# The first token group's routing moved from the start of a routed-experts stage into the attention stage before it

## The chip, the cores and the metric

The kernel runs on one core of a Trainium2 chip. The metric is the device time of one execution in microseconds; less is better. The engines are TensorE (PE, with its weight loads as PEld), VectorE (DVE), ScalarE (ACT), GpSimd (POOL) and SyncE (SP), which here only issues transfers.

## The reference

Four blocks follow each other on x of 32 sequences by 128 tokens by 128 features; each is a cross-attention to a context and a feed-forward part, both added to x with a tanh gate after a layer norm. The kernel's stages 0 to 7 are these eight parts. The change touches stage 2 and stage 3, the second block:

```
x = x + jnp.tanh(g_xattn[1]) * _L1_xattn_ref(_layernorm(x), ctx, ...)   # 16 heads of 8, softmax over 128 keys, then a 2-layer MLP
x = x + jnp.tanh(g_ffn[1]) * _L1_ffn_ref(_layernorm(x), ...)

logits = x @ classifier_weight.T              # 40 experts: 32 routed, 8 identity
scores = softmax(logits)
_, topk_idx = top_k(scores + bias, 6)
topk_w = take_along_axis(scores, topk_idx) * 2.5
out = x * (sum of the weights of the identity experts)
for each of the 32 routed experts:            # intermediate width 64
    gate, up = split(x @ Wgu.T)
    out = out + w[:, None] * (silu(gate) * up @ Wd.T)
```

## The kernel before

x stays on the chip (x_resident), as 8 groups of 4 sequences, 512 tokens each. Each stage is a program block of its own; `end_layer` (L72) closes it with a barrier of all engines. Inside a stage each engine has its own instruction list, written out by hand, and waits on semaphores.

**Stage 2, the attention** (`layer2_attention`). `stream` calls a body for groups 0 to 7 with the group at hand (`at`), the one `before`, the one `after` and the one after that (`after2`). The body has four batches b (one sequence each). TensorE makes scores for batch b + 2, weighs the values of batch b, turns the probabilities of b + 1. VectorE takes the reciprocal of a batch's sums (`invert`, L596), then `shift`: two reduces for the row maxima (L585) and two subtracts (L590) on the scores. ScalarE makes the exponentials, copies the turned probabilities and keeps the outputs; GpSimd multiplies by the reciprocals (L545). In the slots of the batches lie also the norm of `after2` (statistics at b = 1, power on GpSimd at b = 2, normalise at b = 3, turned by TensorE and copied by ScalarE at b = 3), the projections of `after`, and the closing MLP (`hide`, L776, `mix`, L784) and `update` (L603) of `before`. Groups 6 and 7 have no `after2`, group 7 no `after`, so these slots are empty there. All this uses one work bank. After the last group come `hide(LAST)` twice, `mix(LAST)` and `update(LAST)`.

**Stage 3, the routed experts** (`layer3_experts`). `turns` runs over the 8 groups; a group has 16 units u of two experts. TensorE multiplies a unit's gate and up weights with the group's turned normalised rows (L1763), ScalarE applies silu (L1726), VectorE multiplies by up (L1686), GpSimd multiplies by the routing weights of the tokens (L1632), and TensorE, three units later, adds the down-projection into a bank (L1778). GpSimd's operand, `w_spread`, is each expert's row of weights repeated over 64 partitions: the weights are transposed (L1750), copied (L1715), written to a row tensor in DRAM (L1606) and read back with eight broadcast transfers (L1613) in four quarters of four units each; `spread[q]` tells that a quarter is there. The next group's norm (steps 0, 2, 4), router (6), routing chain (7) and spread rows (11) lie inside the group at hand. The first group has none before it: its norm, router, chain of some 25 VectorE instructions and spread stand ahead of everything in the stage. SP issues five weight loads of stage 4 first.

## Time and profile before

| | |
|---|---|
| median of three runs | 2156.19 us (2155.06 to 2162.08) |
| span of the profiled execution | 2160.3 us, 47261 instructions |
| TensorE busy | 1966.5 us, 91% |
| VectorE busy | 1551.1 us, 72% |
| ScalarE busy | 1229.6 us, 57% |
| GpSimd busy | 815.2 us, 38% |
| mean granted TensorE clock | 0.941 |
| stage 2's last update ends, stage 3's first group after it | 933.10 us, to 998.10 us |

The profiled execution's own time is known only as its span, from first to last instruction; it lies 4.1 us above the median of the runs. A busy share is a mean over eight stages with different limits, so what a change in one stage is worth has to be read in the order of time around it. In a timeline row the first number is the start, the second the duration of the merged piece, x the count of instructions in it, and the brackets hold the engine's idle time before it and what ended that.

### The profile page before, as it was taken

What the parts mean: (1) busy time and instruction counts of PE and PEld (TensorE: products, weight loads), DVE (VectorE), ACT (ScalarE), POOL (GpSimd) and SP (SyncE); (2) the same over time, 40 slices, a digit from 0 to 9 for tenths busy, and PEclk for the clock granted to TensorE, in tenths of its full rate; (3) what the DMA queues carried; (4) which work ended last, traced back from release to release, by engine and by line L of the source; (5) the groups of instructions that cost most, each with busy time, mean ns of one, the idle gap of its engine ahead of it and who ended that gap; (6) DMA issues with size and microseconds to landing.
All of it is one profiled execution on the core that took longest, in us unless ns stands there. A gap on an engine that the chain in (4) does not pass through costs nothing. (4 is left out here: it accounts for less than half of the span.)

```text
span 2160.3 us, 47261 instructions
## 1 busy us (share of the span) xinstructions
PE 1966.5 (91%) x18167; PEld 1500.7 (69%) x18167; DVE 1551.1 (72%) x3176; ACT 1229.6 (57%) x2804; POOL 815.2 (38%) x708
## 2 busy tenths in 40 slices
PE   6879999999995999969999995997998999999986
PEld 3669999999894666636666663776685666666676
DVE  6899999999987989835444436765586666666656
ACT  2498888888861777713323323884522666666642
POOL 4344454544461333224445444442000333333333
PEclk7699999999997999979999998997999999999995
DMA  2000000000002000043454330001000000000001
GB/s 89 19 2 14 8 15 8 14 15 8 14 2 81 9 9 6 2 97 79 98 123 97 79 80 19 12 1 56 0 2 8 5 5 5 5 5 5 1 1 41
DMA packets 41566, 61.67 MB, mean 29 GB/s; under 512 B 9624, under 2 KB 18368, under 8 KB 40960
## 3 DMA queue, kind: packets, MB, share of 16 engines
q1 hardware_dynamic: 41344, 58.66, 11.2%
q8 instruction: 146, 2.39, 0.5%
q14 instruction: 76, 0.62, 0.1%
HBM read 56.03 MB, written 2.62 MB: 27 GB/s over the span
## 5 line engine op out<-in xcount | busy, mean ns | idle before, releaser
L916 POOL TENSOR_TENSOR a_probs<-a_probs,a_rsums 128x1024 f32<-128x1024 f32 x64 | 121.4, 1897 | 351.0 <-DVE a_rsums L964 351.0
L1632 POOL TENSOR_TENSOR f_h<-f_gated,f_w_spread 128x512 f32<-128x512 f32 x128 | 161.7, 1269 | 194.6 <-PE f_acc L1778 87.2
L1686 DVE TENSOR_TENSOR f_gated<-f_silu,f_up 128x512 f32<-128x512 f32 x128 | 86.9, 684 | 183.2 <-PE f_up L1763 171.3
L1726 ACT ACTIVATE f_silu<-f_gate 128x512 f32<-128x512 f32 x128 | 76.4, 597 | 230.3 <-PE f_gate L1763 230.2
L2453 ACT ACTIVATE f_combine<-f_logits,f_neg_row_max 128x128 f32<-128x128 f32 x512 | 198.5, 395 | 1.0 <-DVE f_neg_row_max L2308 1.0
L2281 POOL TENSOR_TENSOR f_slot_sum<-f_slot_sum,f_logits 128x512 f32<-128x512 f32 x96 | 122.8, 1279 | 171.7 <-DVE f_slot_max L2387 137.8
L2289 POOL TENSOR_TENSOR f_acc<-f_acc,f_row_factor 128x512 f32<-128x512 f32 x128 | 136.9, 1071 | 62.2 <-ACT f_logits L2460 40.0
L1778 PEld LDWEIGHTS f_acc<-f_down,f_h 128*128 128x128 f32 x1024 | 128.9, 192 | 42.7 <-issue 37.8
L2518 PE MATMUL f_give_bank<-f_y,f_combineT 128*128 128x128 f32 x1024 | 139.3, 279 | 14.8 <-DVE f_y L2357 9.6
L952 DVE TENSOR_REDUCE a_negmax<-a_score_bank 128x8 f32<-128x1024 f32 x64 | 78.2, 1222 | 94.1 <-PE a_score_bank L1105 93.9
L2545 PE MATMUL f_logit_bank<-f_phi,f_xT 128*128 128x128 f32 x1024 | 138.0, 279 | 3.3 <-ACT f_logits L2433 3.3
L2518 PEld LDWEIGHTS f_give_bank<-f_y,f_combineT 128*128 128x128 f32 x1024 | 125.0, 192 | 21.0 <-DVE f_y L2357 17.7
L2507 PE MATMUL f_slot_bank<-f_logits,f_xn 128*128 128x128 f32 x1024 | 136.2, 276 | 1.0 <-DVE f_logits L2379 1.0
L1778 PE MATMUL f_acc<-f_down,f_h 128*128 128x128 f32 x1024 | 131.8, 275 | 2.6 <-POOL f_h L1632 2.6
L1763 PE MATMUL f_gate<-f_xT,f_gate_up 128*128 128x512 f32 x256 | 132.6, 600 | 0.9
L1763 PE MATMUL f_up<-f_xT,f_gate_up 128*128 128x512 f32 x256 | 131.6, 596 | 0.0
L2545 PEld LDWEIGHTS f_logit_bank<-f_phi,f_xT 128*128 128x128 f32 x1024 | 126.8, 195 | 4.5 <-ACT f_logits L2433 3.5
L2373 DVE TENSOR_TENSOR f_logits<-f_logits,f_neg_slot_max 128x512 f32<-128x512 f32 x128 | 127.6, 997 | 2.1 <-ACT f_combine L2453 2.1
L2507 PEld LDWEIGHTS f_slot_bank<-f_logits,f_xn 128*128 128x128 f32 x1024 | 124.5, 192 | 2.3 <-DVE f_logits L2379 1.2
L2493 PE MATMUL f_expert_bank<-f_w,f_slots 128*32 128x128 f32 x4096 | 125.9, 275 | 0.0
L2493 PEld LDWEIGHTS f_expert_bank<-f_w,f_slots 128*32 128x32 f32 x4096 | 108.6, 110 | 7.9 <-issue 0.2
L1030 ACT ACTIVATE a_probs<-a_probs 128x1024 f32<-128x1024 f32 x64 | 67.7, 1059 | 66.5 <-DVE a_probs L955 66.4
(326 smaller groups left out, 4931.4 us busy)
## 6 DMA issues: line engine op xcount, KB each, us to landing
f_w_spread<-f_routing_rows SPq DMA_DIRECT2D x64, 512.0 KB, 10.2
f_w<-in_f_w SPq DMA_DIRECT2D x16, 256.0 KB, 2.5
a_cT<-in_ctxT SPq DMA_DIRECT2D x16, 192.0 KB, 2.7
f_gate_up<-in_f_guT SPq DMA_DIRECT2D x1, 2048.0 KB, 7.9
out<-x_resident SPq DMA_DIRECT2D x8, 256.0 KB, 2.4
c_cT<-in_ctxT SPq DMA_DIRECT2D x8, 192.0 KB, 2.7
a_ctx<-in_ctx SPq DMA_DIRECT2D x8, 192.0 KB, 2.6
f_phi<-in_f_phi SPq DMA_DIRECT2D x1, 1024.0 KB, 5.5
```

The lines of the kernel that those rows point to most:

```text
L916: nc.gpsimd.tensor_tensor(probs[:, u], probs[:, u], rsums[:, u, :].unsqueeze(2).to_broadcast([S, 8, S]), ALU.mult).then_inc(normalised, 1)
L1632: nc.gpsimd.tensor_tensor(h[:, u % KEPT, :], gated[:, u % 2, :], w_spread[:, u // PER, u % PER, :], ALU.mult).then_inc(weighted, 1)
L1763: nc.tensor.matmul(ps[step % 2][:, :], gu_w[:, step, k, :], norm.xT[:, s, :], start=True, stop=True).then_inc(done, 1)
L1778: last = nc.tensor.matmul(acc[s][:, j * D:(j + 1) * D], h[:, u % KEPT, j * S:(j + 1) * S], down_w[:, u, :], start=u == 0 and j == 0, stop= ...
L2281: nc.gpsimd.tensor_tensor(slot_sum[:, :, :], slot_sum[:, :, :] if g > 1 else raw[:, (m - 1) % RING], raw[:, m % RING], ALU.add).then_inc(p ...
L2289: nc.gpsimd.tensor_tensor(acc[:, group(g), :], acc[:, group(g), :], factor[:, m // GROUPS % 3, group(g)].unsqueeze(2).to_broadcast([S, G, D]),
L2373: nc.vector.tensor_tensor(e, e, wide(neg_slot[:, m // GROUPS % 3, :]), ALU.add).then_inc(shifts, 1)
L2453: last = nc.scalar.activation(back[:, m % BACKS, j, :], raw[:, m % RING, j, :], ACT.Exp, bias=neg_row[:, k, b:b + 1], accum_out=row_part[: ...
L2493: last = nc.tensor.matmul(expert_banks[m % 2][rows, j * D:(j + 1) * D], slots[:, m % KEPT, j, rows], w_s[:, k, e, :], start=True, stop=True)
L2507: last = nc.tensor.matmul(slot_bank[:, j * CH:(j + 1) * CH], norm.xn[:, g, j, :], raw[:, m % RING, j, :], start=True, stop=True)
L2518: last = nc.tensor.matmul(give_banks[m % 2][:, j * D:(j + 1) * D], backT[:, m % TURNED, j, :], y[:, m % KEPT, j, :], start=True, stop=True)
L2545: last = nc.tensor.matmul(logit_banks[m % 2][:, j * CH:(j + 1) * CH], norm.xT[:, g, j * S:(j + 1) * S], phi_c[:, c, :], start=True, stop=True)
```

## The change

The routing's tiles, semaphores and steps move out of `layer3_experts` into a class, `Routing`, which both stages use. For the first token group: the statistics and the setup of the chain go to group 6, b = 1, of the attention; the power to b = 2; normalise, turn and copy to b = 3; the router, logit maximum, shift and exponential to group 7, b = 0; the weights to b = 1; their transposes and the copy to b = 3. They use the attention's work bank, so hide(before, 0) of group 7 waits for the shift, and hide(LAST, 0) for the copy of the turned weights. SP then writes the rows and issues the first two of four spread quarters while still in stage 2; the last two are issued first in stage 3, ahead of stage 4's loads. `w_spread` becomes four tiles, two of which are allocated around both stages, and norm6's buffers are allocated later. The body of `vector_weights` is that of `route` before; the stage's other groups do the same steps as before, through the class.

```diff
+class Routing:
+
+
+
+    ER, EZ, TOP, SCALE = 32, 8, 6, 2.5
+    E, PAD = ER + EZ, 8 - TOP
+    CHAIN = 15
...
+    def vector_start(self):
+        self.nc.vector.memset(self.cand[:, :, :], BIG).then_inc(self.chain, 1)
+        self.nc.vector.tensor_scalar(self.gscale[:, :], self.core.gates[:, 5:6], self.SCALE, None, ALU.mult)\
+            .then_inc(self.chain, 1)
+
+    def tensor_router(self, pe, norm, s, it, bank):
+        pe.wait_ge(norm.xT_ready, it + 1)
+        for j in range(G):
+            last = self.nc.tensor.matmul(bank[:, j * self.E:(j + 1) * self.E], norm.xT[:, s, j * S:(j + 1) * S],
+                                         self.rw[:, :], start=True, stop=True)
+        last.then_inc(self.logits_in, 1)
+
+    def vector_logits(self, dve, it, bank):
+
+        logits = bank[:, 0:G * self.E].rearrange("p (j e) -> p j e", j=G)
+        dve.wait_ge(self.logits_in, it + 1)
+        self.nc.vector.tensor_reduce(self.negmax[:, :], logits, AX.X, ALU.max, negate=True).then_inc(self.chain, 1)
+        dve.wait_ge(self.chain, it * self.CHAIN + 3)
+        self.nc.vector.tensor_tensor(self.shifted[:, :, :], logits, self.wide(self.negmax[:, :]), ALU.add)\
+            .then_inc(self.shift_done, 1)
+
+    def scalar_exp(self, act, it):
+        act.wait_ge(self.shift_done, it + 1)
+        self.nc.scalar.activation(self.exps[:, :, :], self.shifted[:, :, :], ACT.Exp).then_inc(self.exp_done, 1)
+
+    def vector_weights(self, dve, s, it):
...
+        dve.wait_ge(self.exp_done, it + 1)
+        nc.vector.tensor_reduce(self.sums[:, :], self.exps[:, :, :], AX.X, ALU.add).then_inc(chain, 1)
...
+        nc.vector.tensor_reduce(self.wz[:, s, :], self.w[:, s, :, ER:], AX.X, ALU.add).then_inc(self.routed, 1)
+
+    def tensor_turn(self, pe, s, it, bank):
+        pe.wait_ge(self.routed, it + 1)
+        for j in range(G):
+            last = self.nc.tensor.transpose(bank[0:self.ER, j * S:(j + 1) * S], self.w[:, s, j, 0:self.ER],
+                                            self.core.ident[:, :])
+        last.then_inc(self.w_turned, 1)
+
+    def scalar_keep(self, act, s, it, bank):
+        act.wait_ge(self.w_turned, it + 1)
+        self.nc.scalar.activation(self.wT[:, s, :], bank[0:self.ER, :], ACT.Copy).then_inc(self.wT_ready, 1)
+
+    def sync_rows(self, sp, i, s, it):
+        sp.wait_ge(self.wT_ready, it + 1)
+        sp.dma_start(self.rows[s], self.wT[:, s, :]).then_inc(self.rows_out[s], 16)
+        sp.wait_ge(self.rows_out[s], i * 16 + 16)
+
+    def sync_spread(self, sp, s, q, place, per):
+
+        half = 128 // 2
+        rows = self.rows[s, 2 * per * q:2 * per * (q + 1), :].rearrange("(p e) n -> e p n", e=2)
+        for e in range(2):
+            sp.dma_start(place[e * half:(e + 1) * half], rows[e].unsqueeze(0).to_broadcast([half, per, N]))\
+                .then_inc(self.spread[q], 16)
...
+                routing.sync_rows(sp, 0, 0, 0)
+                for q, place in enumerate(spread_first):
+                    routing.sync_spread(sp, 0, q, place[:, :, :], 4)
...
+                        if after and not after2 and b == 2:
+                            next_norm.gpsimd_rstd(pool, *FIRST)
...
                             invert(*((at, b - 1) if b else (before, G - 1)))
                         if after2 and b == 1:
                             norm.vector_stats(dve, *after2)
+                        if after and not after2 and b == 1:
+                            dve.wait_ge(updated, 1)
+                            next_norm.vector_stats(dve, *FIRST)
+                            routing.vector_start()
                         if before and b == 3:
                             update(before)
                         if after2 and b == 3:
                             norm.vector_normalise(dve, *after2)
+                        if after and not after2 and b == 3:
+                            next_norm.vector_normalise(dve, *FIRST)
                         batch = batch_at(at, after, b + 2)
                         if batch:
                             shift(*batch)
                         if after and b == 1:
                             bias_values(after, work_bank)
+                        if not after and b == 0:
+                            routing.vector_logits(dve, 0, work_bank)
+                        if not after and b == 1:
+                            dve.wait_ge(routing.held.landed, routing.held.all)
+                            routing.vector_weights(dve, 0, 0)
                 stream(dve, group)
                 invert(LAST, G - 1)
...
+                        if after and not after2 and b == 3:
+                            next_norm.scalar_copy(act, *FIRST)
                         if batch:
                             copy_turned(*batch, 2)
                             copy_turned(*batch, 3)
...
                             exponentiate(*batch)
+                        if not after and b == 0:
+                            routing.scalar_exp(act, 0)
+                        if not after and b == 3:
+                            routing.scalar_keep(act, 0, 0, work_bank)
                 stream(act, group)
...
+                        if not after and b == 0:
+                            pe.wait_ge(routing.held.landed, routing.held.all)
+                            routing.tensor_router(pe, next_norm, 0, 0, work_bank)
...
+                        if not after2 and b == 3:
+                            pe.wait_ge(updated, before[2] + 1)
+                            if after:
+                                next_norm.tensor_turn(pe, *FIRST)
+                            else:
+                                routing.tensor_turn(pe, 0, 0, work_bank)
...
                         if before and b == 1:
-                            if after:
-                                pe.wait_ge(v_ready, after[2] + 1)
+                            pe.wait_ge(*((v_ready, after[2] + 1) if after else (routing.shift_done, 1)))
                             hide(before, 0)
                         if before and b == 2:
                             mix(before)
                 stream(pe, group)
+                pe.wait_ge(routing.wT_ready, 1)
                 for f in range(2):
                     hide(LAST, f)
                 mix(LAST)
...
                 sp.sem_inc(weighted, 2)
+                for q in range(len(spread_first), QUADS):
+                    routing.sync_spread(sp, 0, q, w_spread[q][:, :, :], PER)
                 load_ahead(sp, ahead)
...
+                def spread_routing(i, s, it):
+                    routing.sync_rows(sp, i, s, it)
...
-
-                spread_routing(0, 0, 0, True)
-                turns(sp, lambda i, s, it, nxt: nxt and spread_routing(*nxt, False))
+                        sp.wait_ge(weighted, (it - 1) * STEPS + (q + 1) * PER + 2)
+                        routing.sync_spread(sp, s, q, w_spread[q][:, :, :], PER)
+                turns(sp, lambda i, s, it, nxt: nxt and spread_routing(*nxt))
...
             def _(pool):
-                norm.gpsimd_rstd(pool, 0, 0, 0)
-
...
-                nc.vector.memset(cand[:, :, :], BIG).then_inc(chain, 1)
-                nc.vector.tensor_scalar(gscale[:, :], core.gates[:, 5:6], SCALE, None, ALU.mult).then_inc(chain, 1)
-                dve.wait_ge(weights, LOADED)
...
-                norm.vector(dve, 0, 0, 0)
-                route(0, 0)
...
-                norm.scalar_copy(act, 0, 0, 0)
-                exp_of(0)
-                keep_routing(0, 0)
...
-                pe.wait_ge(weights, LOADED)
...
-                norm.tensor_turn(pe, 0, 0, 0)
-                router(0, 0)
-                turn_routing(0, 0)
...
+                norm3 = Norm(core, weights3, "f1", None, begun_before=True)
+                routing = Routing(core, weights3, held3)
+                spread_first = [core.sbuf(f"f1_w_spread{q}", [128, 4, N], ctx=weights3) for q in range(2)]
```

## Rows read from the trace of the kernel before

**Rows 1.** Windows: length, busy us of PE, PEld, DVE, ACT, POOL; granted clock, DMA.

```profile
921.00:933.00 12.00, 7.60 (x33) 4.35 (x24) 1.60 (x2) 1.76 (x3) 0.46 (x1) 0.63 0.01 1
933.00:948.00 15.00, 3.85 (x17) 3.14 (x17) 6.49 (x36) 0.93 (x2) 1.24 (x2) 0.50 0.19 64
948.00:958.00 10.00, 8.74 (x17) 3.44 (x16) 2.42 (x10) 4.26 (x6) 0.08 (x1) 0.83 0.64 148
```

**Rows 2.** Timeline over the boundary of stage 2 and 3: start us, us, engine.

```profile
932.35 0.75 DVE L603 SCALAR_TENSOR_TENSOR x_resident<-a_work_bank,gates,x_resident 128x512 f32<-128x512 f32 x1 [9.53 <-PE a_work_bank L784]
...
934.32 0.20 DVE L1640 MEMSET f_cand<- 128x168 f32 x1 [1.22 <-PEq L72]
...
942.27 0.33 DVE L1650 TENSOR_REDUCE f_negmax<-f_norm_bank 128x4 f32<-128x160 f32 x1 [3.89 <-PE f_norm_bank L1743]
...
943.36 0.32 DVE L1654 TENSOR_REDUCE f_sums<-f_exps 128x4 f32<-128x160 f32 x1 [0.40 <-ACT f_exps L1711]
...
947.17 1.03 PE L1750 MATMUL f_turn_bank<-ident,f_w 128*32 128x128 f32 x4 [4.93 <-DVE f_w_identity L1674]
...
948.00 1.91 PE L1763 MATMUL f_gate<-f_xT,f_gate_up 128*128 128x512 f32 x2
...
948.85 0.33 SPq L1606 DMA_DIRECT2D f_routing_rows<-f_wT  x1
...
950.50 5.38 SPq L1613 DMA_DIRECT2D f_w_spread<-f_routing_rows  x8
...
951.98 0.69 DVE L1686 TENSOR_TENSOR f_gated<-f_silu,f_up 128x512 f32<-128x512 f32 x1 [4.87 <-ACT f_silu L1726]
...
957.92 1.26 POOL L1632 TENSOR_TENSOR f_h<-f_gated,f_w_spread 128x512 f32<-128x512 f32 x1 [20.68 <-DMA f_w_spread<-f_routing_rows]
```

**Rows 3.** Timeline of TensorE in stage 3, first token group and start of second.

```profile
959.33 1.13 PE L1778 MATMUL f_acc<-f_down,f_h 128*128 128x128 f32 x8 [2.59 <-POOL f_h L1632]
...
963.63 0.63 PE L173 MATMUL f_norm_bank<-ident,f_xn 128*128 128x128 f32 x4 [1.46 <-DVE f_xn L162]
...
998.10 1.02 PE L1763 MATMUL f_gate<-f_xT,f_gate_up 128*128 128x512 f32 x2
```

**Rows 4.** Timeline of VectorE in the attention's last two token groups.

```profile
880.68 2.35 DVE L585 TENSOR_REDUCE a_negmax<-a_score_bank 128x8 f32<-128x1024 f32 x2 [1.27 <-PE a_score_bank L739]
...
894.85 0.75 DVE L603 SCALAR_TENSOR_TENSOR x_resident<-a_work_bank,gates,x_resident 128x512 f32<-128x512 f32 x1 [1.16 <-PE a_work_bank L784]
895.88 2.35 DVE L585 TENSOR_REDUCE a_negmax<-a_score_bank 128x8 f32<-128x1024 f32 x2 [0.28 <-PE a_score_bank L739]
...
907.64 2.36 DVE L585 TENSOR_REDUCE a_negmax<-a_score_bank 128x8 f32<-128x1024 f32 x2 [0.40 <-PE a_score_bank L739]
...
912.18 0.94 DVE L596 RECIPROCAL a_rden<-a_kept 128x128 f32<-128x128 f32 x1
...
919.55 0.75 DVE L603 SCALAR_TENSOR_TENSOR x_resident<-a_work_bank,gates,x_resident 128x512 f32<-128x512 f32 x1 [2.88 <-PE a_work_bank L784]
```

**Rows 5.** Timeline of TensorE at the entry of the last stage.

```profile
2108.69 0.63 PE L1310 MATMUL f_turn_bank<-ident,f_xn 128*128 128x128 f32 x4 [1.52 <-PEq L72]
```

**Rows 6.** Timeline of VectorE in an ordinary token group of the attention.

```profile
837.89 0.75 DVE L603 SCALAR_TENSOR_TENSOR x_resident<-a_work_bank,gates,x_resident 128x512 f32<-128x512 f32 x1 [1.16 <-PE a_work_bank L784]
...
839.59 2.35 DVE L585 TENSOR_REDUCE a_negmax<-a_score_bank 128x8 f32<-128x1024 f32 x2
...
850.85 0.81 DVE L142 BATCH_NORM_STATS2 a_stats<-x_resident 128x6 f32<-128x128 f32 x4
...
852.20 2.36 DVE L585 TENSOR_REDUCE a_negmax<-a_score_bank 128x8 f32<-128x1024 f32 x2
```

**Rows 7.** Timeline of TensorE at the end of the attention.

```profile
923.41 1.42 PE L776 MATMUL a_work_bank<-a_oT,a_w 128*128 128x512 f32 x2 [2.09 <-POOL a_oT L545]
...
925.61 2.08 PE L776 MATMUL a_work_bank<-a_oT,a_w 128*128 128x512 f32 x2 [0.78 <-ACT a_hT L670]
...
928.46 3.78 PE L784 MATMUL a_work_bank<-a_w,a_hT 128*128 128x128 f32 x16 [0.78 <-ACT a_hT L670]
```

More of the change, by code:

```diff
@@ L1560, in _, with layer3_experts @@
                         expand(LEAD + m // 2)
-def layer3_experts(core, held, ahead):
-    nc, ER, EZ, TOP, I, SCALE = core.nc, 32, 8, 6, 64, 2.5
-    E, PAD = ER + EZ, 8 - TOP
-    STEPS, QUADS = ER // 2, 4
+def layer3_experts(core, norm, routing, spread_first, held, ahead):
+    nc, I = core.nc, 64
+    STEPS, QUADS = Routing.ER // 2, 4
     PER = STEPS // QUADS
@@ L1768, in group @@
                         if nxt and step == ROUTER_AT:
-                            router(nxt[1], nxt[2])
+                            routing.tensor_router(pe, norm, nxt[1], nxt[2], norm_bank)
                         if nxt and step == SPREAD_AT:
-                            turn_routing(nxt[1], nxt[2])
+                            routing.tensor_turn(pe, nxt[1], nxt[2], turn_bank)
                         if step >= DOWN_LAG:
```

146 lines of the change are left out of this document (64 added, 82 removed).

## The prediction

> **What bounds the kernel now.** I read the windows around the boundary of stage 2 and stage 3 first, then the timeline of all engines over it, the start of stage 3 on TensorE, and last VectorE's order of work in the attention's ordinary and last groups.
>
> The 15 us after the attention's last update hold almost nothing: TensorE is busy 3.85 us, VectorE 6.49, ScalarE 0.93, GpSimd 1.24, at a granted clock of 0.50 [rows 1]. What runs there is one chain. The update ends at 933.10, VectorE starts the stage at 934.32, the logits' reduction comes at 942.27, the routing weights from 943.36, their transposes at 947.17, the first gate matmul at 948.00, the first row write at 948.85, the spread transfers from 950.50, and GpSimd's first product at 957.92, after 20.68 us idle, released by the spread transfer [rows 2]. TensorE has by then run four units ahead and idles 2.59 us until that product allows the first down-projection, then 1.46 us more for the second group's normalised rows [rows 3]. From there it is continuous: 998.10 is the second group's first gate. So in this stage TensorE sets the end, and what is late at the start is paid in full at the stage's closing barrier.
>
> In the attention the pace is a loop of scores on TensorE and reduce and subtract on VectorE: VectorE's reduce at 907.64 waits only 0.40 us for TensorE's scores, which wait for the subtract before; two batches lie between 895.88 and 907.64, 5.88 us each [rows 4]. VectorE work put there costs only what exceeds such a gap.
>
> **Removed from the start of stage 3.** TensorE's first gate matmul then waits only for a semaphore (gateds) that VectorE raises as it enters; the turned rows exist already. Stage 2's last update to VectorE's first instruction took 1.22 us [rows 2]; at the entry of the last stage, where TensorE also has work ready, it started at the same 2108.69 as that stage's first VectorE work, 1.52 us idle behind the barrier [rows 5]. I take 934.32 plus an estimated 0.2 us of weight load: gate matmul at 934.5 against 948.00, which is 13.5 us. (Between 934.3, no load, and 935.5, a second barrier's length, the bounds.)
>
> The Trainium skill ("Runtime: NRT & Kernel Launch", Instruction fetch mechanics) says that a branch out of the fetched window makes the sequencer stall for a fetch; before, TensorE waited for the norm at this entry and would have hidden it. The page gives no time for it, and the stage entry in [rows 5] shows none worth counting; by that rule the 13.5 would shrink, by the row it does not.
>
> Then the pipe. Before, the fourth unit ended 2.59 us ahead of 959.33 [rows 3], at 956.7, or 8.7 us after the first gate. GpSimd's first product had its other input at 952.67, when VectorE's first gated tile was done [rows 2], and was late at 957.92 only for its transfer. Without that it comes 4.8 us after the first gate, at 939.3, and ends 1.26 us later at 940.6, ahead of the fourth unit's end, now 943.2. Its transfer must land by 939.3. In the tail: transposes at about 921.4 once the last weighing is done, row write 1.68 us later (947.17 to 948.85), spread issue 1.65 later (950.50), landing no more than 7.42 later (957.92) [rows 2]: 921.4 + 1.0 of slip (below) + 10.75 = 933.2. Six microseconds are spare; each microsecond beyond would cost one. Quarters three and four are issued after the barrier, at 934.3; even at twice 7.42 they land at 949, and unit 8, in the middle of a group that took 50.1 us (948.00 to 998.10), comes near 957. So the 2.59 us go. The 1.46 us go too: statistics, GpSimd's power and the normalise of group 1 depend on the first product, now 2.5 us ahead of the fourth unit instead of 2.6 behind the need; even a normalise slowed to 3 us fits. Sum: 13.5 + 2.59 + 1.46 = 17.55 us. The five loads for stage 4 now stand behind four spread issues in SP's queue (5.38 us for eight [rows 2], so under 3), and are for the stage after this one: nothing.
>
> **Added to the attention.** In group 6, batch 1: four statistics and four aggregations. Ordinary groups have the same at this place: 850.85 to the reduce at 852.20, no idle [rows 6], where group 6 had a 1.27 us gap before 880.68 [rows 4]; 1.35 with overlap fits the gap. The memset and the scale behind it (0.20 and 0.10 long, pitch far less) have no cover left: 0.2 us. GpSimd's two instructions (1.24 us [rows 1]) sit between two products a 5.88 us batch apart: nothing, 1.24 if that cover were gone. Batch 3: the normalise between update and reduce. Ordinary group: 837.89 to 839.59, 1.70 us [rows 6]; group 6: 894.85 to 895.88, 1.03 us [rows 4]. Plus 0.67 us, on the loop. Transposes and ScalarE's copy stand where ordinary groups have them: nothing.
>
> Group 7, batch 0: eight router matmuls between two pairs of turns (all of TensorE's moved work is 3.85 us at the 0.50 clock [rows 1], 1.9 at full; I estimate half of it for the router), in the time VectorE takes for its reduce and subtract; the turns behind them come later by a few tenths and the chain over ScalarE's copies may pass some on. I count 0.1. The two logit instructions (0.33 us each, 942.27 [rows 2]) delay the last subtract by 0.3 after the 0.40 us gap, but TensorE has a full queue of turns, weighing, hide and mix then; nothing. Batch 1: the weights, 943.36 to 947.17, 3.8 us [rows 2], behind the last subtract, from 912.2. VectorE has there two reciprocals and then 2.88 us of idle before the update at 919.55 [rows 4]; the late thing is the reciprocal at 912.18, moved to 916, and behind it GpSimd's product and bias. The update of group 6 waits for mix, not for these; VectorE is free by about 918. Hidden, with some 1.3 us spare. Tail: transposes and copy end about 1.3 us after 921.4, hide(LAST) starts only at 923.41, waiting 2.09 us for GpSimd [rows 7]. SP is done issuing by 928, before the barrier.
> Slip: 0.2 + 0.67 + 0.1 = 1.0 us. Lower bound 0; upper bound 4.8, the weights wholly on the path.
>
> **Sum.** 17.55 - 1.0 = 16.5 us. The profiled span is 2160.3, so the changed span should be near 2143.8. The runs' median, 2156.19, is 4.1 us (0.19%) under that span; I take the difference over unchanged: 2139.7 us.
>
> **The clock.** TensorE's granted clock was 0.63 in 921 to 933, 0.50 in 933 to 948, 0.83 in 948 to 958 [rows 1], so about 3.4 us of the stage's first gates ran at 1.2 GHz, 1.7 us lost. The sum keeps that. The tail's second hide (2.08) and mix (3.78) [rows 7] ran at the lower level too, after a 2.09 us idle; the routing transposes (1.03 us at the low clock [rows 2], half at full) now lie in that gap. If they hold the clock at 2.4 GHz, half of 5.86 is won, 2.9 us, about 0.4 of the first hide and the 1.7: 5 us. The other way, TensorE has been slow when stage 3 opens and stays so twice as long: 1.7 us lost.
> The Trainium skill ("TensorE: Matmul & The Clock Gate", What's actually happening) calls the low clock the default, released by activity; that TensorE fell after an idle gap and rose after 948 agrees with it, and it is the rule behind the next rival.
>
> **Rivals.**
> Clock kept (17%): as worked out, 16.5 + 5.0 = 21.5, 2134.7 us. For: less idle in the tail. Against: gaps for ScalarE's rectify follow in the tail as before, and TensorE is idle again over the barrier.
> Routing in the way (10%): the 3.8 us of weights push the late reciprocals, and with them GpSimd's products and the last batches, onto the path. 16.5 - 3.8 = 12.7, 2143.5 us. For: the 1.3 us of spare is small. Against: the idle before 919.55.
> No visible change (4%): TensorE's start moves, but GpSimd's unit 8 waits for quarter three, which is now issued behind the barrier, and gives 12 us back: 4.5 us left, 2151.7 us. That needs a landing at 957 + 12 = 969, 35 us after the issue. For: it is the one part of the spread that is not moved ahead. Against: the first quarter landed in 7.42 [rows 2].
> Slower (3%): the clock stays at 1.2 GHz in the first group, because the stage opens straight behind the slow tail instead of behind a fresh burst. From 959.33 to 998.10 TensorE does 38.8 us of work at full clock [rows 3]; half clock costs as much again. It decides at 33 us beyond the usual ramp; all of the group gives 2139.7 + 38.8 = 2178.5 us. For: in 921 to 933 TensorE was busy 7.60 of 12 us and still fell. Against: in 948 to 958, 8.74 of 10 busy and it rose [rows 1].
>
> **How the numbers follow.** Forecast 66%, own range 2137 to 2143 (slip 0 to 2.7, start 934.3 to 935.5, slow ramp 1.7). For the 8 in 10 it reaches past the clock rival below and the routing rival above, and about 2 us for the spread of runs (2155.06 to 2162.08): 2132 to 2147. Measurement tells 0.3%, 6.5 us, from no change. Faster needs a gain over 6.5: 0.93; within: 0.04; slower: 0.03.
>
> **What would show it.** After: first gate at 934.5 plus the slip, about 935.5; no GpSimd wait for the spread transfer; no idle on TensorE between the fourth unit and the second down-projection; 46.1 us from the first gate to the second group's first, where it was 50.1. In the attention: reduce after update in group 6 near 1.7 us after it, the weights inside VectorE's idle before the last but one update, first hide(LAST) still released by GpSimd. The prediction is wrong if that hide is released by ScalarE's routing copy by more than a microsecond, if the clock row of the first 10 us differs from 0.83, or if GpSimd still waits for the transfer.

## The result, and the profile after

The changed kernel takes 2129.82 us (median of four runs, 2129.33 to 2139.49), the kernel before 2155.62 beside it (four runs, 2152.85 to 2162.08): a ratio of 0.9888, with a 95% interval of 0.9868 to 0.9908. The forecast was 2139.7, in a range of 2132 to 2147: the sign was right, and the measured median lies 2.2 us below the range. A second comparison on another occasion (the second run below) gave 0.9908 (0.9881 to 0.9935), which is 2134.4 against 2156.04 us. Over the ten runs of the changed kernel in these two comparisons the mean is 2134.2 us; over 40 runs of the kernel before, from all comparisons, it is 2155.8. The gain is thus about 21.5 us, larger than the 16.5 forecast. The runs of the kernel before spread over some 12 us, those of the changed kernel over some 18, and the second median and the mean lie inside the range: that the first median lies under it is in part the spread of runs.

The profiled execution of the kernel before was its slowest (2162.08 us); that of the changed kernel is an ordinary one (2130.05). Whole spans can therefore not be set against each other. The stages that the change touches can, since the trace gives each by itself.

First the boundary of the two stages, in windows laid like those of [rows 1]: the 12 us up to just before the end of the attention's last update, then 15 and 10 us. Columns as there.

```profile
915.30:927.30 12.00, 8.07 (x101) 5.63 (x99) 2.33 (x3) 2.58 (x5) 1.77 (x3) 1.00 0.40 92
927.30:942.30 15.00, 13.52 (x49) 7.17 (x50) 7.59 (x19) 5.35 (x8) 7.40 (x7) 1.00 1.07 211
942.30:952.30 10.00, 10.00 (x53) 6.65 (x52) 4.43 (x17) 4.69 (x6) 3.79 (x3) 1.00 0.34 98
```

TensorE is busy 13.52 of the 15 us in which it was busy 3.85, and the granted clock is 1.00 in all three windows, where it was 0.63, 0.50 and 0.83 [rows 1]. The first was forecast. The second was not.

The timeline of the changed kernel over the same stretch:

```profile
918.49 0.61 PE L273 MATMUL a_work_bank<-ident,f_w 128*32 128x128 f32 x4
...
919.75 0.32 SPq L283 DMA_DIRECT2D f_routing_rows<-f_wT  x1
...
920.73 1.10 PE L912 MATMUL a_work_bank<-a_oT,a_w 128*128 128x512 f32 x2 [1.63 <-POOL a_oT L662]
921.40 9.59 SPq L291 DMA_DIRECT2D f_w_spread<-f_routing_rows  x8
...
922.60 1.13 PE L912 MATMUL a_work_bank<-a_oT,a_w 128*128 128x512 f32 x2 [0.78 <-ACT a_hT L800]
...
924.51 2.05 PE L920 MATMUL a_work_bank<-a_w,a_hT 128*128 128x128 f32 x16 [0.78 <-ACT a_hT L800]
926.67 0.75 DVE L722 SCALAR_TENSOR_TENSOR x_resident<-a_work_bank,gates,x_resident 128x512 f32<-128x512 f32 x1 [6.62 <-PE a_work_bank L920]
...
928.54 1.10 PE L1819 MATMUL f_gate<-f_xT,f_gate_up 128*128 128x512 f32 x2 [1.99 <-DVEq L1764]
...
932.58 1.26 POOL L1758 TENSOR_TENSOR f_h<-f_gated,f_w_spread 128x512 f32<-128x512 f32 x1 [11.99 <-DVE f_gated L1773]
...
936.15 1.05 PE L1834 MATMUL f_acc<-f_down,f_h 128*128 128x128 f32 x8
```

and the start of the second token group on TensorE, which answers to the last of [rows 3]:

```profile
973.22 1.02 PE L1819 MATMUL f_gate<-f_xT,f_gate_up 128*128 128x512 f32 x2
```

From the last update's end to the first gate matmul there are now 1.12 us (927.42 to 928.54), where there were 14.90 (933.10 to 948.00, [rows 2]): 13.8 us gone. GpSimd's first product is released by VectorE's gated tile, no longer by the transfer, and the first down-projection follows without an idle. From the first gate to the first down-projection are 7.61 us, where there were 11.33 [rows 3]: 3.7 gone. From there to the second group's first gate are 37.07 us, where there were 38.77: 1.7 gone. In the tail of the attention the second hide and the mix take 1.13 and 2.05 us, where they took 2.08 and 3.78 [rows 7], and first hide to last update is 5.94 us, where it was 8.94: 3.0 gone.

What it cost shows in VectorE's rows of the attention's last two groups, beside [rows 4]:

```profile
891.42 0.75 DVE L722 SCALAR_TENSOR_TENSOR x_resident<-a_work_bank,gates,x_resident 128x512 f32<-128x512 f32 x1 [1.16 <-PE a_work_bank L920]
892.09 1.11 DVE L162 TENSOR_SCALAR f_xn<-x_resident,f_mean_var,f_rstd 128x128 f32<-128x128 f32 x4
893.11 2.35 DVE L704 TENSOR_REDUCE a_negmax<-a_score_bank 128x8 f32<-128x1024 f32 x2
...
909.43 0.31 DVE L247 TENSOR_REDUCE f_sums<-f_exps 128x4 f32<-128x160 f32 x1
...
913.10 1.75 DVE L715 RECIPROCAL a_rden<-a_kept 128x128 f32<-128x128 f32 x2
916.78 0.75 DVE L722 SCALAR_TENSOR_TENSOR x_resident<-a_work_bank,gates,x_resident 128x512 f32<-128x512 f32 x1 [1.93 <-PE a_work_bank L920]
```

Update to reduce takes 1.69 us in group 6, as forecast (1.70). The 3.7 us of the weights (909.43 to 913.10) push the reciprocals back, and VectorE still idles 1.93 us before the update. The first hide of the last group stood 28.56 us behind the update inside group 6 before (894.85 to 923.41) and stands 29.31 us behind it now (891.42 to 920.73); 0.66 us of the difference is the normalise between update and reduce (1.69 against 1.03 us), where 0.67 was forecast. Its slip over the whole kernel is 0.8 us: the traces run 3.5 us apart as the attention starts and 2.7 us apart at that hide (923.41 and 920.73).

The sum of the two stages is 13.8 + 3.7 + 1.7 + 3.0 − 0.8 = 21.4 us.

### The profile page after: what moved, and what is told of

Same layout as the page of the kernel before. It is cut to its first block and busy times, and to the rows that moved or that the text cites. A ratio compares the mean times of both kernels' runs of the same rounds, so it can differ in the third digit from the quotient of the medians.

```text
span 2128.2 us, 47268 instructions
## 1 busy us (share of the span) xinstructions
PE 1944.8 (91%) x18167; PEld 1485.9 (70%) x18167; DVE 1548.2 (73%) x3176; ACT 1228.5 (58%) x2804; POOL 815.2 (38%) x708
```

## The experiments

Two things were to be told apart: whether the excess over the forecast is the clock (the clock theory, "theory C" where the expectations use letters; the other letters are explained in the expectation that uses them), and which of the moved parts the 19.2 us of the experts' stage hang on. "Stage 2" is the attention and "stage 3" the routed experts; stage lengths are from barrier to barrier in the traces. They are what the verdicts rest on, since without an edit stage 2 repeats to 0.5 us and stage 3 to 0.2, while whole times don't. Each variant has one trace, so a stage length is one execution's.

**The same kernels again.** No edit; the baseline of all that follows.

> The kernel before, once more, for its stage lengths and clock. In the first pair of traces stages 2 and 3 got 21.4 us shorter together and the other stages 10.7 us. Theory A (the change acts in stages 2 and 3 alone, the rest is where the low-clock stretches happen to fall): stage 2 and 3 lengths repeat within 2 us (260.3 and 371.3), the other stages move by some microseconds with the length of their low-clock stretches, and the span comes out nearer 2153 than 2160. Theory B (the change also shortens stages 4 to 6): the other stages repeat as in the first trace of before.

> The changed kernel, once more, with its profile. Theory A: stage 2 about 258.1, stage 3 about 352.1, first gate matmul within 0.5 us of the stage's entry, no low-clock stretch over the boundary of stage 2 and 3; time about 2130, ratio 0.988. If the clock over the boundary is a matter of luck, this trace shows a low stretch there and stages 2 and 3 are together up to 5 us longer.

Before: 2153.93 us in one run, with stage 2 0.5 us longer and stage 3 0.2 us longer than in its first profile, and a span of 2152.1 us where the first was 2160.3. After: 2134.4 us over six runs (2128.93 to 2146.69), ratio 0.9908 (0.9881 to 0.9935), stage 2 2.0 us and stage 3 19.2 us shorter than before's. The two traces of the kernel before have the same tail, those of the changed kernel too. That is theory A: the change acts in stages 2 and 3, and the other stages of the kernel before differ between its own two traces by about as much as between the first pair (8.9 us against 10.7).

**The transposes a step earlier.** The routing weights are turned before the last weighing, into a bank of the score turns, and no longer in TensorE's gap ahead of the last hide.

```diff
-                            routing.scalar_keep(act, 0, 0, work_bank)
+                            routing.scalar_keep(act, 0, 0, turn_banks[0])
...
+                        if not after and b == 3:
+                            pe.wait_ge(copies, (at[2] * G + b) * QUADS + QUADS + 2)
+                            routing.tensor_turn(pe, 0, 0, turn_banks[0])
                         weigh(at, b)
...
-                            else:
-                                routing.tensor_turn(pe, 0, 0, work_bank)
```

> The changed kernel with the four transposes of the routing weights moved out of TensorE's idle gap ahead of hide(LAST, 0), to before the last weigh, into a turn bank. Costs 0.45 us of TensorE's path by itself. Theory C (those transposes in the gap keep the clock at 2.4 GHz over the boundary, which is the 5 us that the forecast left out): the clock falls in the tail as in before, stage 2 about 3 us and stage 3 about 2 us longer, 5 us in all, time about 2135. Rival D (the clock stays up because TensorE restarts earlier in stage 3, or by luck; the transposes do nothing): only the 0.45 us, within 1 us of the changed kernel.

Measured: 2136.8 us (2134.52 to 2138.29, five runs), ratio 0.9908 (0.9889 to 0.9928). TensorE at the end of the attention:

```profile
917.13 0.60 PE L273 MATMUL a_turn_bank<-ident,f_w 128*32 128x128 f32 x4
...
921.79 1.10 PE L912 MATMUL a_work_bank<-a_oT,a_w 128*128 128x512 f32 x2 [2.17 <-POOL a_oT L662]
923.66 2.07 PE L912 MATMUL a_work_bank<-a_oT,a_w 128*128 128x512 f32 x2 [0.78 <-ACT a_hT L800]
926.51 3.78 PE L920 MATMUL a_work_bank<-a_w,a_hT 128*128 128x128 f32 x16 [0.78 <-ACT a_hT L800]
...
932.28 1.10 PE L1820 MATMUL f_gate<-f_xT,f_gate_up 128*128 128x512 f32 x2 [1.98 <-DVEq L1765]
```

The slow hide and mix of [rows 7] are back, and stage 2 is 4.0 us longer than the changed kernel's. Of that, 2.7 us lie between the first hide and the last update (8.62 us against 5.94) and 0.4 just ahead of the first hide, the price of the move. The other 0.9 arose in the stage's first groups: in this execution the granted clock also fell in the second token group (a mean of 0.51 over 725.7 to 729.1, 1.00 at this place in the changed kernel), where the code is the same. But the first gate matmuls of stage 3 run at 1.10 us all the same, and stage 3 is 19.2 us shorter than before's as in the changed kernel, where the expectation had it 2 us longer. So the tail's 3 us hang on this half microsecond of transposes, and the start of the experts doesn't depend on the clock that the tail had. The medians of this run and of the changed kernel (2136.8 and 2134.4) lie the right way round, but their ratios to the kernel before are the same: whole times don't show the 4 us by themselves.

**The kernel before, with the gap filled.** Four transposes of an identity, which nothing reads, ahead of the last group's first hide.

```diff
                 stream(pe, group)
+                for j in range(G):
+                    nc.tensor.transpose(turn_banks[0][0:32, j * S:(j + 1) * S], core.ident[:, 0:32], core.ident[:, :])
                 for f in range(2):
                     hide(LAST, f)
```

> The kernel before with four extra transposes of the identity (the same 128x32 shape, results unread) in the same gap ahead of hide(LAST, 0), nothing else. Theory C: the tail runs at 2.4 GHz, stage 2 about 3 us shorter; TensorE then idles over the start of stage 3 and the clock falls there, so stage 3 is as before; time about 3 us under before. Rival D: no difference beyond noise, 2155.

Measured: 2153.02 us (2149.61 to 2159.41, twelve runs), ratio 0.999 (0.9977 to 1.0004).

```profile
918.93 0.61 PE L834 MATMUL a_turn_bank<-ident 128*32 128x128 f32 x4
921.08 1.12 PE L776 MATMUL a_work_bank<-a_oT,a_w 128*128 128x512 f32 x2 [1.54 <-POOL a_oT L545]
922.98 1.12 PE L776 MATMUL a_work_bank<-a_oT,a_w 128*128 128x512 f32 x2 [0.78 <-ACT a_hT L670]
924.88 2.05 PE L784 MATMUL a_work_bank<-a_w,a_hT 128*128 128x128 f32 x16 [0.78 <-ACT a_hT L670]
...
942.68 1.92 PE L1765 MATMUL f_gate<-f_xT,f_gate_up 128*128 128x512 f32 x2
```

Stage 2 is 3.5 us shorter than before's without any of the change, 3.0 of it between the first hide and the last update, so the tail's gain is separate from the moved routing. Stage 3 is 0.4 us longer: the gates at its start are as slow as before.

**That, and stage 3's start filled as well.** 24, 4 and 36 more transposes of the identity around the norm's turns, the router and the routing's turns.

```diff
+                for _ in range(24):
+                    nc.tensor.transpose(turn_bank[:, 0:S], core.ident[:, :], core.ident[:, :])
                 norm.tensor_turn(pe, 0, 0, 0)
+                for _ in range(4):
...
                 router(0, 0)
+                for _ in range(36):
...
                 turn_routing(0, 0)
```

> The kernel before with transposes of the identity (results unread) in the tail's gap and in TensorE's three waits at the start of stage 3 (24, 4 and 36 of 128x128), so that nothing is moved and only TensorE's clock can change. Theory C: clock at 2.4 GHz over the boundary; stage 2 about 3 us shorter, stage 3 about 3 us shorter (turn, router, routing transposes and the first gates at full speed), 6 us in all, time about 2150. Rival D: no change, or slower by fillers that overrun the waits.

Measured: 2152.2 us (2146.68 to 2159.31, twelve runs), ratio 0.9991 (0.9977 to 1.0005).

```profile
938.96 1.02 PE L1771 MATMUL f_gate<-f_xT,f_gate_up 128*128 128x512 f32 x2
...
949.46 1.26 POOL L1634 TENSOR_TENSOR f_h<-f_gated,f_w_spread 128x512 f32<-128x512 f32 x1 [20.01 <-DMA f_w_spread<-f_routing_rows]
...
950.86 2.05 PE L1786 MATMUL f_acc<-f_down,f_h 128*128 128x128 f32 x8 [4.20 <-POOL f_h L1634]
```

and the window behind that wait, columns as in [rows 1]:

```profile
949.80:956.60 6.80, 5.74 (x15) 3.60 (x16) 4.44 (x7) 0.60 (x1) 5.38 (x6) 0.50 1.07 223
```

The first gate matmuls run at the full clock, 1.02 us, and that wins nothing: TensorE waits 4.20 us for the first product instead of 2.59, so that first gate to first down-projection takes 11.90 us, where the kernel before took 11.33. Counted from the last update's end the first gate comes 1.25 us sooner than before (13.65 against 14.90) and the first down-projection 0.7 us (25.55 against 26.23). These 0.7 us come from the turns and the router ahead of the gates, since the way from the routing's turns to the first product is no shorter (10.93 against 10.75 us). They are lost again at once: the clock fell in the longer wait, the first eight down-projections take 2.05 us instead of 1.13, and from there to the second group's first gate are 39.95 us instead of 38.77. Stage 3 is thus 0.5 us longer than before's, stage 2 2.9 us shorter; about 6 us in all had been expected. In the kernel before, the slow first gates were hidden behind the spread transfer.

**The spread late.** The changed kernel, but the row write and all four quarters of the spread are issued as stage 3 opens; norm, router and weights stay in the attention.

```diff
-                routing.sync_rows(sp, 0, 0, 0)
-                for q, place in enumerate(spread_first):
-                    routing.sync_spread(sp, 0, q, place[:, :, :], 4)
...
-                for q in range(len(spread_first), QUADS):
+                routing.sync_rows(sp, 0, 0, 0)
+                for q in range(QUADS):
```

> The changed kernel with the row write and all four spread quarters issued at the entry of stage 3 instead of the first two in stage 2; the weights are still made and transposed in stage 2. Theory E (the early transfers pay only what of their chain sticks out behind TensorE's four units): rows 1.65 us, first quarter at most 7.42 us, so GpSimd's first product waits until about 9.1 us after the entry instead of 4.3, the first down-projection comes 2.7 us later, and the 1.46 us wait for the second group's rows returns: stage 3 is 2.7 to 4.1 us longer, stage 2 unchanged; time 2137 to 2139. Rival F (the early spread is worth as much as its whole chain, 9 us, or nothing, since TensorE runs ahead): stage 3 longer by 9, or by under 1.

Measured: 2140.48 us (2136.32 to 2143.77, four runs), ratio 0.9931 (0.9909 to 0.9953); stage 3 is 4.95 us longer than the changed kernel's.

```profile
932.34 1.10 PE L1817 MATMUL f_gate<-f_xT,f_gate_up 128*128 128x512 f32 x2 [1.98 <-DVEq L1762]
...
941.76 1.26 POOL L1756 TENSOR_TENSOR f_h<-f_gated,f_w_spread 128x512 f32<-128x512 f32 x1 [17.38 <-DMA f_w_spread<-f_routing_rows]
...
943.16 1.13 PE L1832 MATMUL f_acc<-f_down,f_h 128*128 128x128 f32 x8 [3.06 <-POOL f_h L1756]
...
947.48 0.63 PE L173 MATMUL f_norm_bank<-ident,f_xn 128*128 128x128 f32 x4 [1.47 <-DVE f_xn L162]
```

The two idles of [rows 3] are back in full, 3.06 us for the transfer and 1.47 for the second group's normalised rows. So both hang on the first product. That is the prediction's step for the 2.59 and the 1.46, shown by undoing it: the early row write and issue of the first quarters are worth 4.95 us here, somewhat more than the 2.7 to 4.1 expected.

**The weights late too.** As the run before, and the weights, their turn and their copy at stage 3's entry, with only norm and router left in the attention.

```diff
-                            routing.vector_weights(dve, 0, 0)
...
                 dve.sem_inc(updated, 2)
+                routing.vector_weights(dve, 0, 0)
...
-                            routing.scalar_keep(act, 0, 0, work_bank)
...
...
-                                routing.tensor_turn(pe, 0, 0, work_bank)
...
+                routing.tensor_turn(pe, 0, 0, turn_bank)
```

> The changed kernel with only norm, router, shift and exponential in the attention; the routing weights, their transposes, the copy and all transfers are back at the start of stage 3, ahead of the first gate. Theory (the path is the sum of its steps): VectorE 3.8 us plus transposes put the first gate about 5.1 us later, the first quarter lands about 15 us after the entry, the first down-projection comes 8.4 us later than in the changed kernel, with 1.4 us more for the second group's rows: stage 3 longer by 8 to 11 us. Theory C besides: with no transposes in the gap of the tail, the clock falls there, stage 2 about 3 us longer. Together 11 to 14 us, 2145 to 2148. Rival D (the gap does not matter): stage 2 as in the changed kernel or 0.3 shorter.

Measured: 2145.8 us (2140.7 to 2147.3, five runs), ratio 0.9955 (0.9937 to 0.9973); stage 3 is 10.5 us longer than the changed kernel's, stage 2 as long.

```profile
922.70 1.10 PE L904 MATMUL a_work_bank<-a_oT,a_w 128*128 128x512 f32 x2 [2.17 <-POOL a_oT L659]
924.58 1.12 PE L904 MATMUL a_work_bank<-a_oT,a_w 128*128 128x512 f32 x2 [0.78 <-ACT a_hT L794]
...
934.37 1.03 PE L273 MATMUL f_turn_bank<-ident,f_w 128*32 128x128 f32 x4 [5.84 <-DVE f_w_identity L268]
935.20 1.91 PE L1814 MATMUL f_gate<-f_xT,f_gate_up 128*128 128x512 f32 x2
```

The stage's part is as a chain at its entry should be: TensorE waits 5.84 us for the weights, and behind that idle the first gates are slow again, 1.91 us, where they took 1.10 behind an idle of 1.99. The tail is a miss for the clock theory: the gap is unfilled and 2.17 us long, as in the run with the early transposes, and the clock stayed. What an unfilled gap costs is thus not settled by its length.

**Other times for the same gap.** Four, then eight extra VectorE operations (into a scratch tile that nothing reads; four take 0.87 us) in group 6, batch 3, in either kernel, so that the gap comes later and is otherwise as it was.

```diff
+                        if after and not after2 and b == 3:
+                            for k in range(4):
+                                nc.vector.tensor_scalar(scratch[:, k, :], core.X_groups[:, 0, 0, k % G, :], core.gates[:, 1:2],
+                                                        None, ALU.mult)
```

> The kernel before, with four extra VectorE operations on 128 x 128 values (about 0.17 us each, into a scratch tile that nobody reads) in the last group of stage 2 ahead of the last chain of the weights, so that the last groups come some 0.7 us later and the gap of TensorE ahead of the last group's first filler product stays as long as before (2.1 us) and unfilled. Theory C (an unfilled gap of some 2 us there costs the clock; a gap that other TensorE instructions break up does not): the clock falls in the gap as in the kernel before, the filler products take about 2.1 and 3.8 us, stage 2 is 0.7 us longer than before's 260.3 us, the next stage is as before's (371.3). Rival G (when the gap falls, not how long it is or what fills it, decides): at some such offset the clock is kept, products of 1.1 and 2.05 us, and stage 2 is about 2 us shorter than before's.

> As the run with four extra VectorE operations, with eight: the last groups come about 1.5 to 1.8 us later. Theory C: the clock falls, stage 2 is 1.5 to 1.8 us longer than before's 260.3 us. Rival G: it may be kept, and stage 2 is then about 1 us shorter than before's.

> The changed kernel with the same four extra VectorE operations at the same place: the last groups come some 0.7 us later, and the gap ahead of the last group's filler products is still broken up by the routing's transposes. Theory C: the clock is kept, filler products of 1.1 us, stage 2 about 0.7 us longer than the changed kernel's, the next stage the same as there. Rival G: the clock falls at some such offset, the filler products take 2.1 and 3.8 us, stage 2 is some 3.5 us longer and the next stage up to 1.7 us longer than the changed kernel's.

> The changed kernel with eight of them, 1.5 to 2 us later. Theory C: clock kept, stage 2 about 1.5 to 2 us longer than the changed kernel's, the next stage the same. Rival G: the clock may fall, stage 2 then some 4.5 to 5 us longer and the next stage up to 1.7 us longer.

One run each: 2157.78, 2156.95, 2136.9 and 2135.56 us, beside 2159.02 of the kernel before. The two hides of the last group in TensorE's timeline, first the kernel before with four operations:

```profile
920.09 2.04 PE L781 MATMUL a_work_bank<-a_oT,a_w 128*128 128x512 f32 x2 [2.08 <-POOL a_oT L546]
...
922.90 2.08 PE L781 MATMUL a_work_bank<-a_oT,a_w 128*128 128x512 f32 x2 [0.78 <-ACT a_hT L675]
```

the kernel before with eight:

```profile
922.48 1.12 PE L781 MATMUL a_work_bank<-a_oT,a_w 128*128 128x512 f32 x2 [2.08 <-POOL a_oT L546]
...
924.39 1.96 PE L781 MATMUL a_work_bank<-a_oT,a_w 128*128 128x512 f32 x2 [0.78 <-ACT a_hT L675]
```

the changed kernel with four:

```profile
921.88 1.10 PE L917 MATMUL a_work_bank<-a_oT,a_w 128*128 128x512 f32 x2 [1.63 <-POOL a_oT L663]
...
923.76 1.12 PE L917 MATMUL a_work_bank<-a_oT,a_w 128*128 128x512 f32 x2 [0.78 <-ACT a_hT L805]
```

and with eight:

```profile
926.50 1.10 PE L917 MATMUL a_work_bank<-a_oT,a_w 128*128 128x512 f32 x2 [1.63 <-POOL a_oT L663]
...
928.37 1.12 PE L917 MATMUL a_work_bank<-a_oT,a_w 128*128 128x512 f32 x2 [0.78 <-ACT a_hT L805]
```

The clock fell in both with the gap open (2.08 and 1.96 us for the second hide, against 1.12) and stayed in both with it filled. The rival that only the gap's place in time decides (rival G) had these four as its test, and none of them went its way. Stage 2 is 1.0 and 0.1 us longer than before's in the first two, and 0.7 and 2.6 us longer than the changed kernel's in the last two. Over all profiles the count is: gap filled, clock kept in eight of eight (the changed kernel twice, the two fills of the kernel before, the late spread, the two slips here, the last run below); gap open, clock fallen in five of six, the sixth being the run with late weights. Where the clock falls moves too: with four operations the first hide is slow already (2.04 us), with eight only the second (1.12, then 1.96), as in the run with the early transposes. The fill is what goes with a kept clock; that the place of the gap in time has a say where it is open, the sixth run and that shift suggest and don't prove.

**More fills elsewhere.** The changed kernel with 84 and 76 transposes of an identity at the entries of stages 2 and 4, where TensorE waits and the clock is low.

```diff
                 pe.sem_inc(weighed, 2)
+                for _ in range(84):
+                    nc.tensor.transpose(score_bank[:, 0:S], core.ident[:, :], core.ident[:, :])
                 pe.wait_ge(weights, LOADED)
...
+                for _ in range(76):
+                    nc.tensor.transpose(work_bank[:, 0:S], core.ident[:, :], core.ident[:, :])
                 pe.wait_ge(held.landed, held.all)
```

> The changed kernel with transposes of the identity (results unread) while TensorE waits for loads and norm at the entries of stage 2 (84) and stage 4 (76), where its traces show low-clock stretches of 20 us each. If theory C carries over, stages 2 and 4 are each 2 to 5 us shorter, time 2124 to 2130 against 2134. If fillers in one long wait do not hold the clock through the short gaps that follow, under 1 us each.

Measured: 2136.41 us (2133.73 to 2140.93, six runs), ratio 0.9918 (0.9901 to 0.9934). The windows over 20 us at the entries of stage 2 and stage 4, in the changed kernel:

```profile
668.00:688.00 20.00, 8.71 (x28) 5.10 (x28) 12.51 (x36) 2.57 (x4) 2.73 (x6) 0.50 0.62 213
1281.00:1301.00 20.00, 8.11 (x21) 4.61 (x21) 14.50 (x68) 3.16 (x7) 9.76 (x9) 0.53 0.18 40
```

and with the fills:

```profile
668.40:688.40 20.00, 16.20 (x112) 13.99 (x112) 12.89 (x36) 2.46 (x4) 2.73 (x6) 0.83 0.64 217
1281.40:1301.40 20.00, 14.75 (x92) 11.85 (x93) 13.50 (x65) 2.31 (x4) 8.35 (x8) 0.79 0.18 41
```

TensorE's first matmuls of stage 2 that do the stage's work, in the changed kernel:

```profile
678.60 2.07 PE L854 MATMUL a_turn_bank<-a_cT,a_wk 96*128 96x512 f32 x2 [12.93 <-DMA a_mask<-in_a_mask]
```

and behind the fill:

```profile
670.88 11.37 PE L850 MATMUL a_score_bank<-ident 128*128 128x128 f32 x84 [4.91 <-PEq L72]
682.09 1.02 PE L856 MATMUL a_turn_bank<-a_cT,a_wk 96*128 96x512 f32 x2
```

The clock rises early, but the stages are not shorter (+0.6 and −0.3 us, where 2 to 5 us less each had been expected). What such a fill is worth this run doesn't show, for other things lie over it. The 84 transposes took 11.37 us and outlasted the wait that they were to fill: the first working matmul comes 11.59 us behind the stage's barrier instead of 8.41. VectorE's first reduce comes 17.54 us behind the barrier all the same, 1.04 sooner than in the changed kernel, but without a fill it came 16.50 to 18.88 us behind it in other profiles. Then, between 726 and 729.5 us, the clock fell (a mean of 0.53), as it did at this place in the run with the early transposes, and after that group this stage is 0.6 us behind. In stage 4 the first input that VectorE's norm waits for came 1.3 us later than in the changed kernel. No run here beat the changed kernel.

## Why the prediction was off

The moved chain went as the prediction put it:
- The gate matmul came 13.8 us earlier against the update's end, where 13.5 were forecast. TensorE's first matmul stands 1.12 us behind that end, where the prediction allowed 1.4; the 0.2 us that it added for a weight load doesn't show. The Trainium skill's rule of a fetch stall at a branch ("Runtime: NRT & Kernel Launch", Instruction fetch mechanics) would have shown here, if the entry is such a branch, since matmuls are ready there and nothing hides a stall; the row shows none.
- The waits of 2.59 and 1.46 us went, and the run with the late spread brought both back by undoing the early issue alone. The transfer that GpSimd's first product needs was issued at 921.40, and the product was ready to start at 932.4, 11 us later; 7.42 had been enough before [rows 2]. That leaves 3.6 us to spare, not the six of the prediction, because the tail and the first unit were faster than it took them to be.
- The attention slipped by 0.8 us, where 1.0 was forecast, with the weights inside VectorE's idle.
- Waiting for the third quarter ("No visible change") and a slow first group ("Slower") did not occur; nor did "Routing in the way".
- Of the prediction's own signs of being wrong one came: the granted clock of the first 10 us behind the gate is 1.00, not 0.83. And the first gate to the second group's first is 44.7 us, not 46.1.

The step that failed is the one headed "The clock", in its sentence "The sum keeps that". It left the second hide and the mix at 1.2 GHz and 1.7 us of slow ramp in stage 3. Measured, the tail was 3.0 us shorter, and the first gate to first down-projection 3.7 us shorter instead of 2.59, since the first gates took 1.10 us instead of 1.91, and those behind them 1.02 instead of 1.88. That is 3.0 + 1.1 = 4.1 of the 4.9 us between forecast and measured sum; the rest is 0.3 at the entry, 0.2 in the last wait and 0.2 of slip. The rival "Clock kept" had this mechanism, at a chance of 17%. That its total fits to 0.1 us (21.5 against 21.4) is partly luck: it put 3.3 us on the tail and 1.7 on the ramp where 3.0 and 1.1 were measured, and the small terms made up the rest.

Two reasons stood against it in the prediction. One was the short gaps for ScalarE's rectify: at 0.78 us each they are still there, and with the gap ahead of them filled the clock outlasted them in all eight profiles. The other was the idle over the barrier: it was 6.3 us from the end of the mix to the norm's turn in the kernel before (932.24 to 938.53) and is 1.99 us to the first gate matmul now. The clock outlasted that too, and with the early transposes it was up for the first gate even behind a slow tail. The prediction had the shorter idle in its own numbers and did not ask what it does to the clock. That TensorE's clock is low by default and released by activity (the Trainium skill, "TensorE: Matmul & The Clock Gate", What's actually happening) agrees with the rows, and was used too narrowly: the half microsecond of transposes, taken out of the changed kernel and put into the kernel before, is what goes with the tail's clock, apart from the one run in which it held without them; and the short idle at the entry is what goes with the fast gates, which were slow again in the run with the late weights.

The ramp of stage 3 was also valued by a wrong account. It cost the kernel before nothing, because the transfer hid it: with the gates at full clock TensorE only waited longer for the first product (4.20 us instead of 2.59), which hung on the routing's turns. In the changed kernel it would have been on the path, and did not occur. "The sum keeps that" thus counted as unchanged a loss that was not paid before and is not there after.

The excess of the first comparison (25.8 us against 21.4) is not in the two stages, whose lengths repeat. In the changed kernel's two profiles stages 5 and 6, the sixth and seventh barrier-to-barrier stretches, are together 4.8 and 4.6 us shorter than before's, though nothing in them was changed. The windows over 14 us that end 2.6 us ahead of the last stage, in the kernel before:

```profile
2092.00:2106.00 14.00, 9.79 (x80) 8.93 (x81) 1.77 (x3) 4.24 (x7) 1.90 (x1) 0.76 0.01 1
```

in the changed kernel:

```profile
2059.12:2073.12 14.00, 9.54 (x109) 8.26 (x109) 3.59 (x6) 5.27 (x7) 3.11 (x2) 1.00 0.00 1
```

With the early transposes it is 0.76 again.

The clock falls there in some executions and not in others. The two stretches are 4.6 to 4.8 us shorter than before's in both profiles of the changed kernel, with the late weights and with the changed kernel's slip by eight; they are as long as before's (within 0.5 us) with the early transposes, the late spread and the entry fills, in the kernel before again, and in two of its variants; the three profiles left lie between. All of these have the same code there. What decides it was not settled: it may be chance, or the time at which these stages are entered. Much of the spread of a kernel's times goes with the clock too: of the kernel before, the run at 2150.19 us had a mean granted clock of 0.952, that at 2161.57 us of 0.944.

## What to carry to other kernels

When a chain is taken out of an idle stage boundary, price TensorE's clock on both sides: ask of every slow matmul whether it is on the path now or hidden behind a transfer, and whether it will be afterwards. A piece of work that is moved into a gap ahead of TensorE's own tail can be worth several times its length by what it does to the clock (0.61 us against 3.0 here); a filler ahead of matmuls that then wait for a transfer wins nothing, and one that outlasts its wait is itself in the way. And the sum should be checked stage by stage: whole times moved by 10 us between executions of one kernel, the two stages around the change by half a microsecond, if no further fall of the clock lies in them.

## What the runs showed of the hardware

- Four transposes, 0.61 us, that turned a gap of 2.1 us into one of 1.5 to 1.6 went with a clock of 2.4 GHz over the 5.8 us from the first hide to the end of the mix, with gaps of 0.78 us in it, in eight of eight profiles. Without them it fell in five of six.
- Transposes alone bring the clock up: with 84 of them from 670.88 on, at a stage's entry, the mean granted clock of 20 us there was 0.83 instead of 0.50.
- VectorE's normalise of four 128x128 tiles took 1.11 us in the attention (at 892.09 above) and 2.97 to 3.02 for the experts' second group, where two products of GpSimd ran beside it. No run separates the two.
- A stage can open at full speed: 1.12 us from the last update's end to the first gate matmul, at 2.4 GHz.
